# Even and odd heads stacked in separate partition halves for the first attention

## The reference

```
q = einsum('btd,hdk->bhtk', tgt, Wq) + bq      # tgt = layernorm(x), 16 x 112 x 256
k = einsum('bsd,hdk->bhsk', src, Wk) + bk      # src = ctx_1024,     16 x 375 x 256
v = einsum('bsd,hdk->bhsk', src, Wv) + bv
scores  = einsum('bhtk,bhsk->bhts', q, k) * (1/sqrt(16))
weights = softmax(scores)
out = einsum('bhts,bhsk->bhtk', weights, v)
h = out.transpose(0,2,1,3).reshape(B,T,H*Dh);  return h @ Wo + bo
```

## Time and profile before

| what | value |
|---|---|
| median of 3 runs | 982.67 us (980.79 to 982.67) |
| the profiled execution: its own time | 981.99 us |
| its span in the trace | 980.3 us |
| PE busy over the span | 775.7 us, 79% |
| DVE busy | 631.2 us, 64% |
| ACT busy | 483.2 us, 49% |
| POOL busy | 398.7 us, 41% |
| first `maxima` of the first attention | starts at 45.04 us |
| its last `values` and `turn_values` | at 302 us |

### The profile page before, as it was taken

The page is one execution under the profiler, slowest core; times in us unless marked ns, Lnnn a source line. Parts: engine busy times, 40 slices in busy tenths (PEclk is TensorE's granted clock), DMA queues, the critical chain, the costliest instruction groups (busy, mean ns, idle before and its releaser), DMA issues. The chain is left out here.

```text
span 980.3 us, 21981 instructions
## 1 busy us (share of the span) xinstructions
PE 775.7 (79%) x7078; PEld 610.3 (62%) x7093; DVE 631.2 (64%) x1474; ACT 483.2 (49%) x989; POOL 398.7 (41%) x421
## 2 busy tenths in 40 slices
PE   4579999999978298979999999576888547998840
PEld 2256676767757298978777777465777435665420
DVE  8567677777745759974444444468688336666776
ACT  4736556566543367753333332244655126777642
POOL 4268332323300027881000000676766525756455
PEclk9889999999978669999999999689878759999995
DMA  6447222322260227753222221388432212323223
GB/s 156 112 114 175 67 65 57 79 55 65 49 222 1 88 86 267 251 167 116 66 66 67 66 66 55 99 203 200 147 104 64 62 52 71 120 76 91 90 86 101
DMA packets 84517, 101.59 MB, mean 104 GB/s; under 512 B 16518, under 2 KB 70758, under 8 KB 84422
## 3 DMA queue, kind: packets, MB, share of 16 engines
q1 hardware_dynamic: 69526, 68.42, 24.1%
q0 software_dynamic: 12960, 30.74, 11.2%
q10 hardware_dynamic: 1936, 1.17, 0.5%
HBM read 61.03 MB, written 24.38 MB: 87 GB/s over the span
## 5 line engine op out<-in xcount | busy, mean ns | idle before, releaser
L640 DVE TENSOR_REDUCE a_mx<-ps 112x2 f32<-112x750 f32 x128 | 119.8, 936 | 43.2 <-PE ps L323 37.8
L529 ACT ACTIVATE a_Pf<-ps 125x672 f32<-125x672 f32 x128 | 89.8, 729 | 16.9 <-PE ps L271 16.3
L1245 ACT ACTIVATE ps<-ps 128x512 f32<-128x512 f32 (+1 forms) x57 | 38.3, 672 | 96.3 <-PE ps L51 93.1
L323 PE MATMUL ps<-a_stkK,a_stkQ 96*112 96x375 bf16 x256 | 68.1, 349 | 19.4 <-DMA a_stkK<-a_KS 9.6
L51 PE MATMUL ps<-f_w2hi,f_hh 128*128 (+1 forms) x292 | 79.6, 272 | 3.5 <-issue 2.1
L1400 DVE CAST f_hh<-ps 128x512 bf16<-128x512 f32 x41 | 28.4, 692 | 83.2 <-ACT ps L1245 83.2
L51 PE MATMUL ps<-f_xgThi,f_w1hi 128*128 128x128 bf16 x328 | 73.7, 227 | 7.9 <-issue 3.7
L51 PE MATMUL ps<-f_w2lo,f_hh 128*128 (+1 forms) x292 | 79.5, 272 | 0.0
L51 PE MATMUL ps<-f_w2hi,f_hl 128*128 (+1 forms) x292 | 79.5, 272 | 0.0
L51 PE MATMUL ps<-f_xgTlo,f_w1hi 128*128 128x128 bf16 x328 | 70.6, 217 | 0.0
L51 PE MATMUL ps<-f_xgThi,f_w1lo 128*128 128x128 bf16 x328 | 70.3, 217 | 0.2
(11 more groups left out here) (406 smaller groups left out, 2468.7 us busy)
## 6 DMA issues: line engine op xcount, KB each, us to landing
a_raw<-F_w SPq DMA_DIRECT2D x22, 512.0 KB
f_xg<-f_xd SPq DMA_DIRECT2D x75, 128.0 KB
f_yd<-f_yo SPq DMA_DIRECT2D x75, 128.0 KB
f_raw<-F_w SPq DMA_DIRECT2D x14, 512.0 KB
a_ctxF<-ctxT SPq DMA_DIRECT2D x16, 375.0 KB, 3.3
a_cR<-ctx SPq DMA_DIRECT2D x16, 375.0 KB
a_cT_first<-ctxT SPq DMA_DIRECT2D x14, 375.0 KB
f_xd<-a_zero POOLq DMA_DIRECT2D x1, 5248.0 KB, 19.9
```

Of the source, the lines that this page charges most:

```text
L323: last = nc.tensor.matmul(psMX[:T, h, :S], stkQ[0:96, bass.ds(n.b, 1), j // JJ, j % JJ, h * T:(h + 1) * T].rearrange("p o q -> p (o q)"), ...
L529: nc.scalar.activation(Pf[:, s % PB], psST[:C, s % 2, :SC, :QW], ACT.Exp).then_inc(exp_done, 1)
L640: nc.vector.reduce_max(mx[:, n.odd, 2 * j:2 * j + 2], psMX[:T, :, :S], AX).then_inc(mx_red, 1)
L1245: nc.scalar.activation(hidden(s), hidden(s), ACT.Silu).then_inc(act_done, 1)
```

## The change

- `stkQ` and `stkK` get 128 partitions in two halves. Even heads use partitions 0 to 49, odd heads 64 to 113: 48 rows of features (`KEYS`) and two for the maximum. Nothing is masked any more: a query is stored once.
- `maxima` keeps two matmuls per pair, now over 48 partitions each, one in each half. `scores` has six matmuls over 50 partitions with 112 columns instead of three over 98 with 224. The exponential takes the factor 1/4 as its scale.
- Keys: each copy moves 16 partitions instead of 32, so 24 instead of 12 per batch; SP issues 8 (`K_SP`), POOL 16 (`K_POOL`). `place_maxima` needs 4 DMAs per half batch instead of 2.
- Queries: ACT writes one high part straight from PSUM, DVE one low part, per projection; the intermediate copy, the mask and its preparation go. Stacking the first four batches takes 12 DMAs on SP and 12 on POOL, the other twelve batches 24 on POOL (8 in each of three iterations).
- PE computes `scores` right behind `maxima`, ahead of `keys` or `vals`, and its program has no loop any more. The programs of the other engines keep theirs.

SP has 8 and 4 + 4 where it had 6 and 2 + 2. The core of the diff:

```diff
-        stkQ = sb("stkQ", [98, B, KD, JJ, QW], BF16)
-        stkK = sb("stkK", [98, 4, KD, JJ, S], BF16)
+        SIDE, KEYS, DOT = P // 2, 3 * DH, 3 * DH + 2
+        stkQ = sb("stkQ", [P, JJ, B, KD, T], BF16)
+        stkK = sb("stkK", [P, 4, JJ, KD, S], BF16)
+        QS = sb("QS", [P, 2, B, KD, T], BF16)
...
-        PIECES = [(jj, a, part) for a, part in ((0, 0), (1, 1), (2, 0)) for jj in range(JJ)]
-        K_IN = len(PIECES) // 2 * 16
+        PIECES = [(jj, h, a, part) for a, part in ((0, 0), (1, 1), (2, 0)) for jj in range(JJ) for h in range(2)]
+        K_SP, K_POOL = PIECES[0::3], PIECES[1::3] + PIECES[2::3]
+        SP_IN, POOL_IN = 16 * len(K_SP), 16 * len(K_POOL)
+        Q_PIECES = [(jj, h, i, part) for jj in range(JJ) for i, part in ((0, 0), (1, 0), (2, 1)) for h in range(2)]
...
                 def place_maxima(n, half):
                     sp.wait_ge(turn_free, 2 * n.b + half + 1)
-                    for part in range(2):
-                        sp.dma_start(stkQ[96 + part:97 + part, bass.ds(n.b, 1), half].rearrange("o b j (h q) -> o (b j h) q", q=T),
-                                     cneg[:, n.odd, half, part, :]).then_inc(c_in[half][n.odd], 16)
+                    for h in range(2):
+                        for part in range(2):
+                            row = SIDE * h + KEYS + part
+                            sp.dma_start(stkQ[row:row + 1, :, bass.ds(n.b, 1), half, :].rearrange("o j b q -> o (j b) q"),
+                                         cneg[JJ * h:JJ * (h + 1), n.odd, half, part, :]).then_inc(c_in[half][n.odd], 16)
...
-                        for jj, a, part in PIECES[0::2]:
-                            sp.dma_start(stkK[32 * a:32 * a + 32, w.slot, :, jj, :], KS[32 * jj:32 * jj + 32, w.odd, part])\
-                                .then_inc(k_sp[w.slot], 16)
+                        for jj, h, a, part in K_SP:
+                            sp.dma_start(stkK[SIDE * h + DH * a:SIDE * h + DH * (a + 1), w.slot, jj],
+                                         KS[2 * DH * jj + DH * h:2 * DH * jj + DH * (h + 1), w.odd, part]).then_inc(k_sp[w.slot], 16)
...
                     for c in range(SC):
-                        last = nc.tensor.matmul(psST[:C, j % 2, c, :QW],
-                                                stkK[:, b.slot, j // JJ, j % JJ, c * C:(c + 1) * C],
-                                                stkQ[:, bass.ds(b.b, 1), j // JJ, j % JJ, :].rearrange("p o q -> p (o q)"),
-                                                start=True, stop=True)
+                        for h in range(2):
+                            side = slice(SIDE * h, SIDE * h + DOT)
+                            last = nc.tensor.matmul(psST[:C, j % 2, h, c * T:(c + 1) * T],
+                                                    stkK[side, b.slot, j % JJ, j // JJ, c * C:(c + 1) * C],
+                                                    stkQ[side, j % JJ, bass.ds(b.b, 1), j // JJ, :].rearrange("p o q -> p (o q)"),
+                                                    start=True, stop=True)
...
                     at_least(pe, mx_red, n.b * NJ + j)
                     for h in range(2):
+                        side = slice(SIDE * h, SIDE * h + KEYS)
                         last = nc.tensor.matmul(psMX[:T, h, :S],
-                                                stkQ[0:96, bass.ds(n.b, 1), j // JJ, j % JJ, h * T:(h + 1) * T].rearrange("p o q -> p (o q)"),
-                                                stkK[0:96, n.slot, j // JJ, j % JJ, :], start=True, stop=True)
+                                                stkQ[side, j % JJ, bass.ds(n.b, 1), j // JJ, :].rearrange("p o q -> p (o q)"),
+                                                stkK[side, n.slot, j % JJ, j // JJ, :], start=True, stop=True)
...
+                        if b is not None:
+                            scores(b, s)
                         if w is not None and s % 2 == 0:
                             (keys if s < 4 else vals)(w, s // 2 % 2)
-                        if b is not None:
-                            scores(b, s)
...
-                run(pe, emit)
+                emit(None, None, ring(0), ring(1), None, None)
+                for b in range(B + 1):
+                    p, b, n, w = (ring(b + d) if 0 <= b + d < B else None for d in (-1, 0, 1, 2))
+                    emit(p, b, n, w, None, None)
...
-                            nc.scalar.activation(Pf[:, s % PB], psST[:C, s % 2, :SC, :QW], ACT.Exp).then_inc(exp_done, 1)
+                            nc.scalar.activation(Pf[:, s % PB], psST[:C, s % 2, :, 0:SC * T], ACT.Exp, scale=DH ** -0.5).then_inc(exp_done, 1)
...
                 def queries(g):
...
+                        nc.scalar.activation(QS[:, 0, rows(g), m, :], queried(n).rearrange("p (b q) -> p b q", q=T), ACT.Identity,
+                                             bias=bias[:, 0, m:m + 1]).then_inc(q_hi, 1)
```

More of the change, by code:

```diff
@@ L149, in l0_attention @@
         one = sb("one", [4 * KD * JJ * S // ONES, ONES], BF16)
-        psST = k.ps[:, 0:4, :].rearrange("p (u b) (two n) -> p u (b two) n", u=2, two=2)
+        psST = k.ps[:, 0:4, :].rearrange("p (u h) n -> p u h n", u=2)
         psMX = k.ps[:, 4:6, :]
@@ L206, in run, with stack_queries @@
                 emit(at(-1), at(0), at(1), at(2), some(3), some(4))
[L208 to L215, removed]
+        def stack_queries(eng, batches, pieces, stacked):
+            for jj, h, i, part in pieces:
+                eng.dma_start(stkQ[SIDE * h + DH * i:SIDE * h + DH * (i + 1), jj, batches],
+                              QS[2 * DH * jj + DH * h:2 * DH * jj + DH * (h + 1), part, batches]).then_inc(stacked, 16)
         with nc.Block() as block:
@@ L256, in _ @@
                 sp.wait_ge(one_set, 1)
-                for r in range(2):
-                    sp.dma_start(stkK[96 + r:97 + r].rearrange("o a t j s -> o (a t j s)"), one[:]).then_inc(ones_in, 16)
-                stack_queries(sp, 0)
+                for h in range(2):
+                    for r in range(SIDE * h + KEYS, SIDE * h + DOT):
+                        sp.dma_start(stkK[r:r + 1].rearrange("o a j t s -> o (a j t s)"), one[:]).then_inc(ones_in, 16)
+                sp.wait_ge(q_lo, KD)
+                stack_queries(sp, slice(0, GB), Q_PIECES[0::2], first_q[0])
                 emit(None, None, None, ring(0), (ring(1),), (ring(2),))
@@ L333, in turn_maxima @@
                     at_least(pe, o_free, n.b * NH - (2 if half else 4))
[L334 removed]
+                    nc.tensor.transpose(psT[:HH, :], mx[:, n.odd, half].rearrange("p h j -> p (h j)"), k.ident[:T, :T]).then_inc(turn_full, 1)
                 def turn_tokens(g):
@@ L374, in _ @@
                 vals(ring(0), 1)
-                pe.wait_ge(q_copied, KD * NG)
-                pe.wait_ge(ones_in, 32)
-                pe.wait_ge(q_in[0], 3 * JJ * 16)
+                pe.wait_ge(q_lo, KD * NG)
+                pe.wait_ge(ones_in, 64)
+                for stacked in first_q:
+                    pe.wait_ge(stacked, 16 * len(Q_PIECES) // 2)
                 def emit(p, b, n, w, x, l):
@@ L595, in queries @@
                 def queries(g):
-                    if g == QN:
-                        dve.wait_ge(q_in[0], 3 * JJ * 16)
                     for m in range(KD):
-                        for h in range(2):
-                            dve.wait_ge(q_hi, 2 * (KD * g + m) + h + 1)
-                            nc.vector.scalar_tensor_tensor(masked[g][:, 1, :, m, h, :], qf[:, m].rearrange("p (b q) -> p b q", q=T),
-                                                           pair[:, h:h + 1], masked[g][:, 0, :, m, h, :],
-                                                           ALU.mult, ALU.subtract).then_inc(q_lo, 1)
+                        n = KD * g + m
+                        dve.wait_ge(q_hi, n + 1)
+                        nc.vector.scalar_tensor_tensor(QS[:, 1, rows(g), m, :], queried(n).rearrange("p (b q) -> p b q", q=T),
+                                                       bias[:, 0, m:m + 1], QS[:, 0, rows(g), m, :],
+                                                       ALU.add, ALU.subtract).then_inc(q_lo, 1)
                 def low_keys(w, i):
```

81 lines of the change are left out of this document (27 added, 54 removed).

## The result

The changed kernel is slower: median 1046.24 us (1038.48 to 1051.0, 4 runs) against 981.73 us (974.58 to 982.67, 4 runs), ratio 1.0651, 95% interval [1.061, 1.0693]. The forecast was 1058 us, with a range of 1006 to 1075 us. The profiled execution is the shortest of the four, 1038.48 us; its span is 1036.7 us where before had 980.3, so 56.4 us are to be found in the trace.

A forecast was written before the change was run, and what follows sets the result against it. Predicted bound: the closed chain of key copies, not PE. Fourteen turns at 20.3 instead of 14.92 us add 75.3 us; with -0.7, +2.3 and -1 that is +75.9 on 981.99, forecast 1058 us, range 1006 to 1075.

The forecast's parts named there:

- What bounds it: Attention iterations: the chain through the key copies, with 1.5 us of slack, sets the turn, though PE looks like the bound.
- POOL's issues: Key copies on POOL: price hardly depends on size, 0.524 us each, fifteen more issues after the first 7.9 us.
- Rivals 2 and 3: Key copies: cheap POOL issues leave SP's queue last, 1003 us, chance 0.11; or PE stays the bound, 953 us, chance 0.11.
- The chain: First maxima to next: 7.6 us to low part, 0.66 to POOL, 7.9 issues, 2.2 landing, 18.4 us against 14.92.
- The clock: PE's clock falls after idle waits in three turns of four: 1.95 us more, 20.3 us a turn.
- rival 1: PE's clock holds in the waits for key copies: 1032 us; chance 0.30 together with the rival of halves not running side by side.
- The share of turns: Attention turns in which PE's clock falls: three in four, within 18.4 us if never and 21.0 if always.
- PE's work: Scores and maxima both halve, 2.4 us off PE per iteration, less 0.5 us for changes; PE done at about 13.0 us.
- rival 4: Array halves don't run side by side, six narrow scores matmuls stay 0.29 us; chance 0.30 together with the clock holding.
- rival 3: Cheap issues or shorter chain leave PE the bound, 13.0 us a turn, 953 us; chance 0.11.
- Around them: Outside the 14 turns: first maxima -0.7 us, iteration without scores +2.3, the end -1, PE without a loop nothing.
- The sum: Whole kernel: 75.3 - 0.7 + 2.3 - 1 = +75.9 us on 981.99, 1057.9 us, median forecast 1058 us.

The follow-up runs named there:

- Experiment 1: Kernel before with only its 12 key copies cut into 24 of 16 partitions, 8 on SP and 16 on POOL: 1055.06 us, ratio 1.0817.
- experiment 6: Keys and values projected one iteration earlier: changed kernel 978.20 us, ratio 1.0001; kernel before 0.9991; kernel before with split key copies 1.0053.
- experiment 3: Changed kernel with 8 key copies of 48 partitions instead of 24 of 16, not computing the reference: 968.50 us, ratio 0.9927.
- experiment 5: Changed kernel with 15 unread filler matmuls on PE ahead of each iteration's first maxima: 1021.23 us, ratio 1.0444.

## Why the prediction was right, and where its sizes were off

**What bounds it.** Right for the changed kernel. The closed chain from one first `maxima` to the next sets its turn, and PE's 14.45 of 14.97 us was not the number to go by. Experiment 1 lengthens the chain alone and loses 8.2%; experiment 6 takes it off the path and the loss is gone. In the kernel before, the chain cost next to nothing (0.9991 without it): it was the next in line, not the bound.

**POOL's issues.** Right in kind: half the bytes cost nearly the full price, 0.484 us where the copies of twice the size cost 0.536. The price taken, 0.524, was 0.04 us too high, 0.6 us over fifteen issues. The step that drew the price of a run from the query copies was too timid: in experiment 1 the same bytes in the same 16 rows, but in two runs each, cost 0.504, and in experiment 3 a copy of 48 rows, three times the bytes, cost 0.504 too. Rivals 2 and 3 needed 0.40 and 0.30 us and fell with it.

**The chain.** 18.4 us forecast, 17.47 measured at full clock (experiment 5). Over the turn shown there it is 7.26 us of issues for 7.9, 1.7 us from the last issue on for 2.2, and 7.4 us to the low part for 7.6; with 0.7 us to POOL's first copy that is 17.0 us, and the longer turns of that kernel make the average. So 0.9 us a turn, 13 us in all, is this term's error.

**The clock.** Right that it falls in most turns, and that this belongs in the forecast; rival 1 (1032 us) left it out. The term was 1.95 us a turn and measures 1.45, 7 us in all. The share of turns was taken too low, three in four: the clock is low at or just behind the start of all fourteen. Four of them still start at the full clock and take 17.7 to 18.2 us, the others mostly 18.9 to 20.6. It was the price of a fall that was taken too high: the second key projection, which the forecast put in the low clock, mostly runs at full. In the turn from 177.39 it starts at 182.79, in the one from 195.60, where the clock is still at 0.50 between 199.60 and 201.60, at 201.84, and in both its matmuls take 0.32 to 0.33 us. The Trainium skill, TensorE: Matmul & The Clock Gate, section HAM oscillation, describes this pattern, a wait for a DMA in each step behind which the clock has to rise again every time; this trace agrees, with 0.50 behind the wait at 177.39.

**PE's work.** The step that both kinds of matmul halve was wrong. It did not matter for the time, since PE was not the bound. At full clock:

```profile
169.81 0.37 PE L326 MATMUL ps<-a_stkK,a_stkQ 48*112 48x375 bf16 x2
170.01 0.33 PE L273 MATMUL ps<-a_stkQ,a_stkK 50*125 50x112 bf16 x6
...
171.58 0.33 PE L273 MATMUL ps<-a_stkQ,a_stkK 50*125 50x112 bf16 x6
171.84 0.32 PE L51 MATMUL ps<-a_wv_hi,a_ctxH 128*125 128x256 bf16 x1
```

A pair of `maxima` takes 0.20 us from start to start, between the 0.16 forecast and the 0.32 of before. Six `scores` take 0.26 to 0.32 us, where three of twice the width took 0.29. So the time of rival 4 held for `scores` and not for `maxima`. Whether its reason held too, halves that run one after the other, is not shown. The six also need six weight loads instead of three, on which PEld works 0.35 us, and no run tells the two apart:

```profile
169.86 0.35 PEld L273 LDWEIGHTS ps<-a_stkQ,a_stkK 50*125 50x125 bf16 x6
```

PE's busy time in a turn at full clock goes from 198.25 / 14 = 14.16 us to 12.7, not by 1.9 us. The forecast of 13.0 us for a turn that PE bounds, in rival 3, would not have come true either: with the copies off the path it is 14.3 us (experiments 3 and 6), because PE, ACT and DVE hand the values to one another and PE idles 1.6 us of it.

**Around them.** First `maxima` -0.5 us (forecast -0.7), iteration without scores +1.6 (+2.3), the rest -0.7 (-1), the loop nothing (nothing). The rest is a sum of two parts, though: from the last first `maxima` to the first matmul behind the attention it is 36.1 us instead of 32.4, and everything behind that is 4.4 us shorter, with the same work; why, no run shows. In the last iteration PE waits 3.06 us for `cneg` behind the fill, where it was 2.32.

**The sum.** On the span 1056 us were forecast and 1036.7 measured. Of the 19.5 us between them 14 x (20.3 - 18.92) = 19.3 us lie in the turn, two thirds of it in the chain and one third in the clock. The median of the runs lies 8 us over the profiled one, so it misses by 12 us. The sum itself has a slip: 1057.9 and 0.7 us are 1058.6, so 1059 us. Both errors lie on the same side and the measured time comes out between the forecast and rival 1 (1032 us); the range of 1006 to 1075 us would have held rival 1's time as well, so it is experiment 5 and the clock's rows, not the time, that tell the two apart.

## What to carry to other kernels

Before narrowing matmuls, look for the closed chain that runs from one iteration's first instruction to the next one's, and count every DMA issue on it at the full price that such an issue has in the trace, here 0.48 to 0.54 us for 24 to 72 KB: ten more of them outweighed all that PE gained. Hold the slack against what is added: 1.5 us stood against 4.6 us of issues. One more iteration between producer and consumer took the whole loss away at no cost that the times show. And look at what the clock does in an added wait: here, with waits of 2.6 to 4.8 us in each turn, it was a third of the loss.

## What the runs showed that I had not expected

- Matmuls in the two halves of the partitions gain only in part: 0.20 instead of 0.32 us for two of 375 columns, nothing for six of 112. Whether the width, the weight loads or the place of the outputs decides was not tried.
- Work that nobody reads paid twice: fifteen filler matmuls a turn gave 2.1 points, and six in each empty place of three iterations half a point (1.0001 to 0.9947, by intervals that overlap a little).
- PE can fall to half clock without any long wait: in experiment 6 it fell behind 2 us in which PE was busy 0.98 us, with no single wait over 0.85 us in the 12 us before, and stayed low for more than 48 us, in which PE was busy 39.74.
- A DMA at the end of a program holds up all engines if the block waits for it: held back to 293.5 us, the fill of 19.8 us cost the kernel before 2%.
